# A four-layer graph network on 4096 nodes: 28 of layer 1's first 32 tiles set between the steps of layer 0's last gate

## The reference

```
# layer 0, its last part (h_attn = attention, hs = state branch, h_enh = feed-forward branch)
comb = concatenate([h_attn, hs], axis=1)
g = sigmoid(silu(ln(comb @ g1_w + g1_b)) @ g2_w + g2_b)
x = x + ln(g * h_attn + (1 - g) * hs + h_enh)
# layer 1
h = relu(layernorm(x))
agg = (adj @ h) / deg
x = x + agg @ W.T + b
```

## Time and profile before

| | us |
|---|---|
| median of 3 runs | 2451.36 (2449.09 to 2451.63) |
| the profiled execution, its time | 2449.79 |
| its span | 2448.1 |
| PE busy | 2246.1 (92% of the span) |
| DVE busy | 1810.1 (74%) |
| ACT busy | 1372.0 (56%) |
| POOL busy | 111.5 (5%) |

### The profile page before, as it was taken

How to read it: one execution, slowest core, us unless ns; L and a number is a source line. 1 busy time by engine, 2 the same in 40 slices (tenths; PEclk the granted TensorE clock), 3 DMA queues, 4 the chain that set the end, 5 groups by cost and what they waited for, 6 DMA issues and landing times. The chain is left out here.

```text
span 2448.1 us, 45783 instructions
## 1 busy us (share of the span) xinstructions
PE 2246.1 (92%) x17180; PEld 1704.3 (70%) x17180; DVE 1810.1 (74%) x2893; ACT 1372.0 (56%) x2132; POOL 111.5 (5%) x124
## 2 busy tenths in 40 slices
PE   5899999999999974999978899999699999999998
PEld 4677777867778653888867777777356666666667
DVE  6967879787787843111139999999598988998896
ACT  6655465564655634666645545555355655565556
POOL 2000000010010100000000000000000000000000
PEclk9899999999999986999999999999899999999999
DMA  7544141431411102222211221221211111111000
GB/s 175 108 61 55 42 78 44 78 58 55 78 43 45 35 35 78 86 87 80 88 49 48 73 64 61 68 70 59 74 44 35 44 48 35 44 52 48 27 31 27
DMA packets 63222, 147.77 MB, mean 60 GB/s; under 512 B 10055, under 2 KB 14810, under 8 KB 62045
## 3 DMA queue, kind: packets, MB, share of 16 engines
q1 hardware_dynamic: 56749, 111.62, 14.4%
q0 software_dynamic: 5760, 33.56, 8.3%
q10 hardware_dynamic: 560, 0.52, 0.1%
HBM read 170.82 MB, written 41.96 MB: 87 GB/s over the span
## 5 line engine op out<-in xcount | busy, mean ns | idle before, releaser
L1876 PE MATMUL bank<-VB,ph 128*128 128x257 f16 x2048 | 518.5, 278 | 74.5 <-ACT ph L1756 27.6
L1877 PE MATMUL bank<-VB,ph 128*128 128x257 f16 x2048 | 517.1, 277 | 0.0
L192 PE MATMUL bank<-s_row,kT_hi 128*128 128x512 f16 x1024 | 306.0, 381 | 8.2 <-DMA s_row<-qT_d 6.3
L1387 PE MATMUL bank<-VA,ph 128*128 128x257 f16 x1024 | 280.7, 274 | 7.1 <-DVE VA L1057 7.1
L1880 PE MATMUL bank<-VB,pl 128*128 128x257 f16 x1024 | 286.1, 279 | 0.0
L1876 PEld LDWEIGHTS bank<-VB,ph 128*128 128x128 f16 x2048 | 202.3, 99 | 117.3 <-ACT ag L1777 29.5
L2515 PE MATMUL bank<-VA,ph 128*128 128x257 f16 x1024 | 280.7, 274 | 3.0 <-ACT w_later_hi L2376 2.4
L2517 PE MATMUL bank<-VA,pl 128*128 128x257 f16 x1024 | 280.3, 274 | 0.0
L1389 PE MATMUL bank<-VA,pl 128*128 128x257 f16 x1024 | 280.3, 274 | 0.0
L1388 PE MATMUL bank<-VA,ph 128*128 128x257 f16 x1024 | 280.3, 274 | 0.0
L2516 PE MATMUL bank<-VA,ph 128*128 128x257 f16 x1024 | 280.3, 274 | 0.0
(11 more groups left out here) (333 smaller groups left out, 4596.4 us busy)
## 6 DMA issues: line engine op xcount, KB each, us to landing
mask<-mask_d SPq DMA_DIRECT2D x256, 256.0 KB, 2.7
mask_d<-in_adj POOLq DMA_DIRECT2D x8, 2048.0 KB, 23.3
xg<-x SPq DMA_DIRECT2D x16, 512.0 KB, 4.3
x<-xo POOLq DMA_DIRECT2D x16, 512.0 KB, 2.9
xg<-in_x SPq DMA_DIRECT2D x8, 512.0 KB, 12.9
w_d<-wr SPq DMA_DIRECT2D x8, 512.0 KB, 2.6
f<-w_d SPq DMA_DIRECT2D x8, 512.0 KB, 14.1
x<-xg SPq DMA_DIRECT2D x8, 512.0 KB, 3.9
```

The costliest lines, as they stand in the source:

```text
L192: last = nc.tensor.matmul(out_ap, st, mv, start=(i == 0), stop=(i == len(todo) - 1))
L1387: nc.tensor.matmul(acc, ph[:, u % HR, c], v_row(V, 0, t), start=(t == 0), stop=False)
L1876: nc.tensor.matmul(acc, p_hi, v_at(V, 0, t), start=first, stop=False)
L1877: last = nc.tensor.matmul(acc, p_hi, v_at(V, 1, t), start=False, stop=final and not weighted)
```

## The change

Rounds 8 and 9 are gone. In their place stands a written order of the same steps for each engine, with 28 tiles of layer 1's group 0 (quads 0 to 6, NEXT = 7) between them:

- PE: `next_tiles` makes the tiles (8 matmuls of 257 columns each, into banks 0 to 3), ACT casts their masks (`next_masks`) into layer 0's ring `ph` of 8 buffers, SP loads 7 more mask quads. A tile of quad q waits for the `VB` rows of group q (`V_lo`); in layer 0's own V_low the two memsets now stand ahead of the increment.
- The last gate's half 0 has banks CD throughout and half 1 has AB; half 1 takes `fey` and `feT` in place of `TH` and `sT`. The attention is transposed first, inside `project_out`. Both first products stand one behind the other.
- The last group's `wr` stays in SBUF and is read from there (`fuse`), without the store to `w_d` and the load back.
- W2, W1, Wv and `a` are loaded in layer 0 into the place of weights that are used up (`w_dense`). Wq and Wk are loaded after the first mask; their transposes and product stand in layer 1's last `part` (`pe_beside` and its like), in banks 0 to 2. Nothing else of the later layers moves: layer 3's `ph` gets another address.
- Layer 1's prologue is one quad (skip = 7) with two short steps behind it (`act_between`, `dve_between`).

The core of the diff:

```diff
+                    def next_masks(t0, t1):
+                        for t in range(t0, t1):
+                            u = G * T + t
+                            n = u // R
+                            act.wait_ge(s_mq[n % MS], 16 * (n // MS + 1))
+                            act.wait_ge(summed.sem, summed.upto(u - HR))
+                            nc.scalar.copy(ph[:, u % HR, :], mask[:, n % MS, (u % R) * GW:(u % R + 1) * GW]
+                                           ).then_inc(high.sem, 1)
...
+                    def next_tiles(t0, t1):
+                        for t in range(t0, t1):
+                            u = G * T + t
+                            pe.wait_ge(high.sem, high.upto(u))
+                            if t % R == 0:
+                                pe.wait_ge(V_lo.sem, V_lo.upto(t // R))
+                            if t == 0:
+                                pe.wait_ge(scaled.sem, scaled.upto(G * R - 1))
...
+                    project_out(G - 1, lambda: last_turn_c(0))
+                    next_tiles(0, 2)
+                    last_turn_c(1)
+                    next_tiles(2, 5)
+                    last_gate_one(0)
+                    last_gate_one(1)
+                    last_turn_gate(0)
+                    next_tiles(5, 9)
+                    last_turn_gate(1)
+                    next_tiles(9, 11)
+                    last_gate_two(0)
+                    next_tiles(11, 13)
+                    last_gate_two(1)
+                    next_tiles(13, NEXT * R)
...
+                    def load_later():
+                        sp.wait_ge(out_made.sem, out_made.upto(G - 1))
+                        for name, src in (("W2", "L2_gnn_W"), ("W1", "L1_gnn_WT"), ("Wv", "L3_gnn_Wv")):
+                            sp.dma_start(later(name)[:, :, 0:D], a[src].rearrange("(k p) n -> p k n", p=P)
+                                         ).then_inc(s_later, 16)
+                        sp.dma_start(vecs[:, :], a["L2_gnn_a"].partition_broadcast(P)).then_inc(s_later, 16)
...
+                skip = 0 if weighted else Q - 1
-                    for q in range(Q):
+                    for q in range(skip, Q):
...
                     for q in range(Q):
                         part(eng, G - 1, q)
+                        if beside is not None:
+                            beside(q)
```

More of the change, by code:

```diff
@@ L583, in first_layer @@
             MS = 3
+            NEXT = Q - 1
             PR = 4
@@ L952, in _ @@
                     gam_row(0)
-                    for i in range(G + 2):
+                    for i in range(G):
                         d, f, z = i, i - 1, i - 2
@@ L1556, in _, with last_gate_two @@
+                    def last_gate_two(j):
+                        pe.wait_ge(sT_lo.sem, sT_lo.upto(2 * (G - 1) + j))
+                        pe.wait_ge(gsilued.sem, gsilued.upto(2 * (G - 1) + j))
+                        for r in range(2):
+                            last = products(pe, cell((CD, AB)[j], r),
+                                            [(cols(last_sT[j], k, r), w("g2", k)) for k in range(HK)], "g2")
+                        last.then_inc(g2_made.sem, 1)
                     pe.wait_ge(reded.sem, reded.upto(0))
@@ L1561, in _ @@
                     pe.wait_ge(gam_rowed.sem, gam_rowed.upto(0))
-                    for i in range(G + 1):
+                    for i in range(G):
                         d, f = i, i - 1
@@ L1708, in one_columns, with groups @@
                         nc.vector.memset(view.rearrange("p (t w) -> p t w", w=VW)[:, :, D:D + 1], value)
-                def groups(eng, quad, part, make=None, between=None):
-                    for q in range(Q):
+                def groups(eng, quad, part, make=None, between=None, beside=None):
+                    for q in range(skip, Q):
                         if make is not None:
@@ L1733, in quad @@
                                      ).then_inc(s_mask[q % MS], 16)
-                    groups(sp, quad, work["sync"], work.get("sync_make"))
+                    for i in range(MS if skip else 0):
+                        sp.sem_inc(s_mask[i], 16 * len(range(i, skip, MS)))
+                    groups(sp, quad, work["sync"], None, work.get("sync_between"))
                 @block.gpsimd
@@ L1790, in _ @@
                         gam_row(0)
-                    groups(act, quad, part, make if weighted else work["act_make"])
+                    groups(act, quad, part, make if weighted else None, work.get("act_between"), work.get("act_beside"))
                 @block.vector
@@ L1852, in _ @@
                         dve.wait_ge(omega_s.sem, omega_s.upto(0))
-                    groups(dve, quad, part, None if weighted else work["dve_make"], one_columns if weighted else None)
+                    groups(dve, quad, part, None, one_columns if weighted else work["dve_between"], work.get("dve_beside"))
                 @block.tensor
@@ L1905, in _ @@
                             gam_rows(q)
-                    groups(pe, quad, work["pe"], make if weighted else work["pe_make"])
+                    groups(pe, quad, work["pe"], make if weighted else None, None, work.get("pe_beside"))
             loaded[0] += G * Q // MS
```

479 lines of the change are left out of this document (312 added, 167 removed).

## The result

The changed kernel takes 2406.84 us, median of four runs (2404.54 to 2411.17); the kernel before, beside it, took 2451.0 (2449.09 to 2451.63). The ratio is 0.9825, 95% interval 0.9809 to 0.984: faster by 44.2 us. The profiled execution took 2404.54 us, the lowest of the four; its span is 2402.9, against 2449.79 and 2448.1.

What follows compares the result with a forecast made beforehand. PE was taken to bound the kernel except in a hole before layer 1, set by a four-engine chain. Group 1 starting at 943.3 instead of 989.5 saves 46.2: 2449.8 - 46.2 + 0.3 = 2404 us, range 2398 to 2418.

Steps and rivals of the forecast that it cites:

- The first product: Last gate on PE: first product starts at 888.0, 3.4 us earlier than before; both halves' products end at 899.3.
- DVE in half 1's way by 1 us: Last gate on DVE: group 6's x statistics hold up half 1's shift for about 1 us.
- step 4: Last gate after the first products: DVE becomes the chain, its list through half 1's shift ending at 903.4.
- The last tanh: End of the gate on ACT: last tanh starts at 915.3 instead of 927.91, 12.6 us earlier.
- a tile stands before a step by over 1 us: Sign that the forecast is wrong: in the gate, a moved tile delays a step that others wait for this long.
- From the last tanh to `V_low`: End of layer 0: the old trace's 16.8 us stay, so group 7's `V_low` ends at 932.2, 12.5 earlier.
- The block's start: Start of layer 1: with the mask loaded first, PE starts 3.8 us behind `V_low`, where it was 10.7.
- The restart: Layer 1's four remaining tiles: half clock for 5.5 us after PE's pause, 6.2 us in all, group 1 at 943.3.
- Layer 1 and its tail: Layer 1's groups stay 37 us apart (259.0 for seven); leftover weight preparation in its last part costs 0.3 us.
- The rival that was given most: Gate: tiles cost the chain what its own banks save, `V_low` stays at 944.7, 33.7 us won, 2416; 10%.
- step 3: Gate: both first products back to back end at 899.3; half 1's wins 12 us, 2.3 of them by full clock.
- The loss of layer 1's clock: Rival: without rest for PE the chip lowers layer 1's clock; at 0.80 the kernel takes 2468; 2%.

Runs made afterwards that it cites:

- shift_first: Changed kernel with group 6's x statistics behind half 1's shift on DVE instead of ahead of it; 2404.28 us in one run.
- chain_order: Changed kernel with five places in the gate's written order exchanged, among them the casts of tiles 15 and 16 moved behind the last tanh; 2406.97 us.
- gate_no_tiles: Changed kernel without the 28 moved tiles; layer 1 makes all 32 tiles of group 0 in its prologue; 2433.47 us.
- early_loads_only: Kernel before with only the early weight loads and the changed layer 1 code, all eight quads in the prologue, old gate; 2443.72 us.
- mask_early: Changed kernel with quad 7's mask, Wq and Wk loaded in layer 0 too; 2402.68 us.
- chain_cast_ahead: chain_order with the cast of tile 15 alone put back ahead of half 1's silu; 2407.39 us.
- last_x_first: Changed kernel with all tiles behind half 1's second product, casts from the ninth behind the last tanh, x store and load ahead of four mask loads; 2415.83 us.
- both_cast_ahead: mask_early and chain_order together, with the cast of tile 15 put back ahead of half 1's silu; 2398.53 us.

## Why the prediction was right

The forecast was 2404 for the profiled execution, which took 2404.54; the median, 2406.84, is 1.3 us over the 2405.5 given for it. Part of this closeness is luck: counted from the scaling of the rows, 44.7 us were won where 45.9 (46.2 less 0.3) were forecast, and the scaling came 0.5 us earlier in this trace. Step by step, against the marks it named:

1. **The first product** starts 11.62 us behind the scaling of the rows, exactly as laid out, and both are done after 22.8 us (22.9 laid out). Full clock, as assumed: the window shows 1.00, not only over 0.9.
2. **DVE in half 1's way by 1 us**: shown by shift_first, 1.06. The rest of step 4 was 0.5 us too short: DVE came to half 1's statistics at 899.66, 23.8 us behind the scaling where 23.1 was laid out, while PE's products had been done since 898.7. (The sum in step 4 makes 903.3, not 903.4.)
3. **The last tanh** 12.1 us earlier, where 12.6 was laid out. This is the 0.5 us of step 4; it stays far from the bound of 2 us that was set for jitter and handovers. Two things on this stretch were wrong. PE should have been idle for 0.2 us at most until 905; it waited 1.69 us for half 1's `gy`, and the layout itself has 1.2 there (tiles 5 to 8 end at 903.7, `gy` at 904.9). The granted clock stayed at 1.00 all the same. And the prediction named as a sign of being wrong that a tile stands before a step by over 1 us. One does, by 1.2 us (0.9 laid out): DVE has the last cut of half 1 ready at 911.07, and PE comes to the second product at 912.27, behind tiles 11 and 12. DVE's timeline, then PE's:

```profile
909.84 1.23 DVE L1220 TENSOR_TENSOR feT_lo<-fey,feT_hi 128x1024 f16<-128x1024 f32 x1 [2.65 <-ACT feT_hi L1024]
```

```profile
912.16 0.27 PE L1729 MATMUL bank<-VB,ph 128*128 128x257 f16 x1
912.27 0.27 PE L192 MATMUL bank<-w_gate_hi,feT_hi 128*128 128x256 f16 x1
```

4. **From the last tanh to `V_low`**: 17.0 us, laid out as 16.9. Of the 7 us of cover for the x load, the load itself takes 3.2 (914.72 to its landing), so 3.5 were spare in front of DVE's sum at 921.45. In chain_order the load left 3.65 us later and DVE wanted it 2.4 us earlier, counted from the scaling: it waited 2.52 us.
5. **The block's start**: 4.6 us from `V_low` to the first matmul, where 3.8 was laid out. SP issued the mask load 0.6 us behind `V_low`, not 0.3, and it landed 3.35 us after its issue, not 2.8; this is inside the bound of 6.6.
6. **The restart**: mis-sized. It was taken as 5.5 us of half clock, as in the trace before; it was 2.7. First matmul to group 1 took 6.2 us (7.3 laid out): 1.4 us less by the clock, and 0.35 more because PE waited 1.24 us for the scaling of group 0, not 0.89. So the start of group 1 is right to 0.3 us by luck: the chain (0.5), the way to `V_low` (0.1) and the block's start (0.8) were longer than laid out, the restart 1.1 shorter.
7. **Layer 1 and its tail**: the tail cost 0.2 us for the 0.3 taken. But the seven groups, taken as unchanged, take 0.7 more, and what lies behind layer 1 another 0.3. They are the whole difference between the 45.9 us won up to group 1 and the 44.7 up to the end.

The rival that was given most, that the tiles cost the chain what its banks save, is refuted by gate_no_tiles: the chain is 2.9 us shorter with the tiles. The prediction had most of this in its step 3, as 2.3 us from full clock; it did not say that the tiles are what buys them. That is also why a tile can stand 1.2 us in front of a step and the chain is still shorter. The loss of layer 1's clock did not come (1.00 over 259 us). PE's clock in the hole did fall in gate_no_tiles (0.78), where the tiles are missing.

**The 0.12 us a group.** Six of the seven groups take 37.23 us after and 37.12 before (the last 37.05 and 37.06), and DVE starts its reciprocal later behind the same last matmul: 0.55 us behind its start for 0.43. DVE's timeline of before, then of after:

```profile
1025.91 0.36 DVE L1827 RECIPROCAL rden<-bank 128x1 f32<-128x1 f32 x4 [3.34 <-PE bank L1877]
```

```profile
1016.88 0.37 DVE L2052 RECIPROCAL rden<-bank 128x1 f32<-128x1 f32 x4 [3.46 <-PE bank L2102]
```

gate_no_tiles has the long groups (260.46 for seven), early_loads_only the short ones (259.74), and mask_early 260.44. So it comes neither with the tiles nor with layer 1's changed code, but with the new gate code ahead of it; what in that code does it was not tried and stays open.

## What to carry to other kernels

Work of the next stage that PE must do anyway, set into the gaps of a chain of small steps, can shorten the chain too, because it keeps the granted clock up: here 2.9 us beside the 24.6 us of the tiles themselves. A cast's place in ACT's order also sets when a buffer is free, when the load into it leaves SP, and when everything behind that load leaves: before moving a step, follow the queue of the engine that waits for it (half a microsecond of cast moved here cost 2.4 us). And after the move look at the gap that is left: with its load moved up as well it fell from 8.5 to 3.3 us, the clock no longer fell, and 2398.5 us beat the changed kernel.

## What the runs showed of the hardware

- The time at half clock after a pause doesn't follow from the pause's length. PE's timelines give 5.5 us after 27.6 us of idle (before), 4.2 after 22.7 (gate_no_tiles), 2.7 after 8.46 (after), 3.6 after 8.45 (shift_first), 5.4 after 7.0 (chain_cast_ahead), 4.2 after 4.7 (last_x_first), none after 3.25 (both_cast_ahead). A restart taken from one trace is good to 3 us of half clock, 1.5 us of time.
- A wait of SP for a semaphore held the DMAs behind it that were themselves ready: in chain_order group 6's x store left at 915.28, 0.37 us behind the mask load that waited for a cast, and in last_x_first, where it stands ahead of that load, at 901.38. The Trainium skill, which tells it in its section on GpSimd's DMAs ("DMA: Bandwidth & Descriptors", Anatomy of one DMA), puts the wait at the same place: it happens on the issuing sequencer, not in the DMA engines.
- Layer 1's loop lost 0.12 us a group with no change in its own code, as told above; the cause is open.
